# Splitting the query loads from the key loads in layer 1's attention, re-ordering the experts' set-up, and moving a gating product from GpSimd to VectorE

## What is computed

```
h = layernorm(x) * (1 + ca) + sa
x = x + ga * attention(h)
h = layernorm(x) * (1 + cb) + sb
x = x + gb * ffn(h)
```

```
norms = jnp.linalg.norm(out, axis=-1)
denom = jnp.maximum(norms.mean(axis=(0, 2)), 1e-05)
proj = (einsum('bhtk,hkd->bhtd', out / denom, Wo) + bo) * gate_val ; proj.sum(axis=1) / H
...
x_attn = layernorm(x) @ attn_w + attn_b + x
g = x_attn.reshape(2, 8, tpe, D)              # 512 tokens for each of 8 experts
y = gelu(g @ w1 + b1) @ w2 + b2
out = gelu(y @ next_w + next_b)
```

## Time and profile before

| | |
|---|---|
| runs | 2066.65, 2069.05, 2069.82 us; median 2069.05 |
| profiled execution | 2068.8 us, its span 2067.0 us |
| granted TensorE clock, mean | 0.944 |
| busy: TensorE / VectorE / ScalarE / GpSimd | 1851.6 / 1314.4 / 1180.1 / 601.1 us |
| attention of layer 1 | about 1255 to 1729 us |
| experts | 1730 us to the end |

### The profile page before, as it was taken

One profiled execution on the slowest core, in us unless ns is written; L12 is line 12 of the kernel. 1 busy time (PEld: TensorE's weight loads), 2 busy tenths in 40 slices (PEclk: granted clock), 3 DMA queues, 4 the chain that ended last, 5 costly groups with the idle time before them and its releaser, 6 DMA issues. The chain is left out here.

```text
span 2067.0 us, 29571 instructions
## 1 busy us (share of the span) xinstructions
PE 1851.6 (90%) x10317; PEld 752.9 (36%) x10317; DVE 1314.4 (64%) x2607; ACT 1180.1 (57%) x1622; POOL 601.1 (29%) x736
## 2 busy tenths in 40 slices
PE   4789999998879999999999987899999985699998
PEld 3323333322234444444444442233333221354443
DVE  5479888888643553553544524888888771757572
ACT  4268788876742432433323323888888665567663
POOL 5657777662110000000001013111111000354654
PEclk8589999999999999999999996999999996799999
DMA  3344554444260000000000031333433304323310
GB/s 114 62 89 118 133 135 108 121 123 102 95 238 11 11 21 2 21 22 1 22 25 22 21 51 42 52 62 73 72 73 62 62 11 149 113 92 111 124 62 31
DMA packets 119666, 147.92 MB, mean 72 GB/s; under 512 B 19810, under 2 KB 102868, under 8 KB 117460
## 3 DMA queue, kind: packets, MB, share of 16 engines
q1 hardware_dynamic: 119508, 145.79, 27.2%
HBM read 100.34 MB, written 45.14 MB: 70 GB/s over the span
## 5 line engine op out<-in xcount | busy, mean ns | idle before, releaser
L824 DVE TENSOR_REDUCE A_M<-A_SM 128x1 f16<-128x512 f32 x1024 | 657.4, 684 | 154.1 <-PE A_SM L1039 152.0
L590 ACT ACTIVATE A_P<-A_ST 128x1024 f32<-128x1024 f32 x512 | 523.5, 1025 | 146.9 <-PE A_ST L1055 143.8
L1039 PE MATMUL A_SM<-A_KT,A_QS 48*128 48x512 f16 x1024 | 358.7, 405 | 59.6 <-DVE A_M L824 53.4
L1582 PE MATMUL B_PA<-B_Hh,B_wh 128*128 128x512 f16 x1024 | 388.4, 379 | 0.0
L1582 PE MATMUL B_PA<-B_Hl,B_wh 128*128 128x512 f16 x1024 | 388.2, 379 | 0.0
L1501 ACT ACTIVATE B_af<-B_PA,B_sv 128x512 f32<-128x512 f32 x192 | 131.9, 687 | 354.8 <-PE B_PA L1582 354.7
L1055 PE MATMUL A_ST<-A_QS,A_KT 49*128 49x512 f16 x1024 | 304.8, 394 | 7.3 <-DMA A_QS<-A_rows 7.2
L1072 PE MATMUL A_AV<-A_P,A_V 128*32 128x512 f32 x2048 | 283.7, 627 | 4.6 <-ACT A_P L590 4.0
L1039 PEld LDWEIGHTS A_SM<-A_KT,A_QS 48*128 48x128 f16 x1024 | 85.1, 94 | 451.6 <-DVE A_M L824 383.0
L1545 DVE TENSOR_SCALAR B_Hh<-B_af 128x512 f16<-128x512 f32 x128 | 58.4, 456 | 281.4 <-ACT B_af L1501 281.4
L1296 POOL TENSOR_TENSOR B_hl<-B_hf,B_hh 128x512 f16<-128x512 f32 x14 | 16.2, 1156 | 519.2 <-ACT B_hh L1312 519.2
(11 more groups left out here) (346 smaller groups left out, 3191.3 us busy)
## 6 DMA issues: line engine op xcount, KB each, us to landing
D_w_st<-in_we_dram SPq DMA_DIRECT2D x16, 1024.0 KB, 5.0
qk<-A_tr SPq DMA_DIRECT2D x58, 256.0 KB, 2.4
A_KT<-qk SPq DMA_DIRECT2D x96, 128.0 KB, 4.5
A_QS<-qk SPq DMA_DIRECT2D x96, 128.0 KB, 5.0
A_w_st<-in_w_ffn_dram SPq DMA_DIRECT2D x32, 352.0 KB, 3.3
A_QS<-A_rows SPq DMA_DIRECT2D x512, 0.5 KB
w_hi<-A_f_hi SPq DMA_DIRECT2D x32, 176.0 KB, 3.4
w_lo<-A_f_lo SPq DMA_DIRECT2D x32, 176.0 KB, 3.5
```

The lines of the kernel that those rows point to most:

```text
L590: nc.scalar.activation(P[:, st, 2 * pair:2 * pair + 2, :], ST[:, u % 2, :, :], ACT.Exp, scale=1.0 / math.sqrt(HD)).then_inc(exp_s, 1)
L824: nc.vector.tensor_reduce(M[G % 2][:, o:o + 1], SM[:, n % 2, :], AX, ALU.max, negate=True).then_inc(max_s, 1)
L1039: nc.tensor.matmul(SM[:, n % 2, :], QS[b % 2][r, 2 * g + pair, tt * 128:tt * 128 + 128], KT[b % 2][r, 2 * g + pair, :], start=True, stop=T ...
L1582: ins = nc.tensor.matmul(out, a, c, start=start and kt == 0 and n_ == 0, stop=stop and kt == kts[-1] and n_ == len(ops) - 1)
```

## The change

Three things change. In AT1, the six query loads of a batch stand at slots 17, 17, 18, 18 (high halves) and 20, 20 (low halves), the six key loads at 23, 23, 24, 24 and 25, 26; each load waits for its own store, and the semaphores hi_st and lo_st become four. Batches 0 and 1 have places of their own in a table that stays. In the experts, the gate of the head outputs is folded into D_rsc (gsc times rsc) and no longer into the weights; the weights are split in three separate pieces; the row of biases is made on two partitions at once (a matmul with two equal columns, a scale that is 0 on the first partition), so the DMA to the second partition is gone; and SyncE issues the load of y ahead of the weights. In `body`, the product of `finish` is taken by VectorE (`gated`), for both q around D_x, GpSimd keeps the sum, both of them ahead of `add_tokens`; D_y2l is no longer interleaved with `add_tokens`; behind the last expert VectorE takes the sum too.

```diff
@@ -127,7 +127,7 @@
                        H0=39, H1=41, H2=49, H3=51, HIGH=(49, 49, 50, 50, 52, 52, 53, 53), LOWS=(56, 56, 57, 57)))
 AT0 |= OUT | dict(P0=(50,), P1=(52,))
 AT1 = placed(-48, dict(STAT=(-38, -37, -35, -34), AGG=-33, ROOT=-32, XN=(-26, -24, -22, -18), T0=-1, T1=1, HH=(0, 2), HL=(1, 3),
-                       QK0=4, QK1=10, QK2=12, QK3=18, V0=20, V1=26, HIGH=(23, 23, 24, 24, 24, 24, 25, 25), LOWS=(25, 25, 26, 26)))
+                       QK0=4, QK1=10, QK2=12, QK3=18, V0=20, V1=26, HIGH=(23, 17, 23, 17, 24, 18, 24, 18), LOWS=(25, 20, 26, 20)))
 AT1 |= OUT
...
-                             ).then_inc(hi_st if which in (KH, QH) else lo_st, 16)
+                             ).then_inc((kh_st, qh_st, kl_st, ql_st)[which], 16)
...
-                sp.wait_ge(hi_st, 32 * (n + 1))
+                sp.wait_ge((kh_st, qh_st)[i % 2], 16 * (n + 1))
...
+            def load_tokens(e):
+                if e >= 2:
+                    sp.wait_ge(x3_s, 2 * (e - 1))
+                q0, q1, t_ = halves(e)
+                for a, q in enumerate((q0, q1)):
+                    sp.dma_start(x2t[e % 2][:, 2 * a:2 * a + 2, :], d["x2_tok"][q, t_, :].rearrange("(t p) c -> p t c", p=128)
+                                 ).then_inc(x_ld[e % 2], 16)
+
+            def load_x(e, y_only=False):
...
+                if not y_only:
+                    load_tokens(e)
...
+            sp.dma_start(gates[:, :], d["gate"].partition_broadcast(128)).then_inc(c_ld[1], 16)
             sp.dma_start(hsel[:, :, :], d["head_of"]).then_inc(c_ld[0], 16)
-            sp.dma_start(gates[:, :], d["gate"].partition_broadcast(128)).then_inc(c_ld[1], 16)
+            sp.dma_start(gcol[:, :], d["gate"].unsqueeze(1)).then_inc(c_ld[3], 16)
+            load_x(0, True)
+            sp.dma_start(wsm[:, :, :, :], d["w_small"].rearrange("a (k p) n -> p a k n", p=128)).then_inc(c_ld[4], 16)
             sp.dma_start(bo[:, :], d["bo"]).then_inc(c_ld[2], 16)
-            sp.dma_start(gcol[:, :], d["gate"].unsqueeze(1)).then_inc(c_ld[3], 16)
-            sp.dma_start(wsm[:, :, :, :], d["w_small"].rearrange("a (k p) n -> p a k n", p=128)).then_inc(c_ld[4], 16)
+            sp.dma_start(rowf[:, 1, :], d["next_b"].partition_broadcast(2)).then_inc(c_ld[7], 16)
             sp.dma_start(vec[:, :, :], d["vec"].rearrange("a p f -> p a f")).then_inc(c_ld[5], 16)
-            sp.dma_start(rowf[:, 1, :], d["next_b"].unsqueeze(0)).then_inc(c_ld[7], 16)
-            load_x(0)
+            load_tokens(0)
             load_rows(0)
             load_w(0, 0)
             load_w(0, 1)
             sp.dma_start(eb[:, :, :], d["eb"].rearrange("e p f -> p e f")).then_inc(c_ld[6], 16)
-            sp.wait_ge(row_low, 1)
-            sp.dma_start(row2[1:2, :, :], rowl[:, :, :]).then_inc(row_ld, 16)
...
+                    if m == E8 - 1:
+                        sp.wait_ge(x4_last, q_ + 1)
+                    else:
+                        sp.wait_ge(x4_s, 2 * m + q_ + 1)
...
-            def finish(m, qs):
-
-                for q in qs:
+            def finish(m):
+
+                for q in range(2):
                     v = xo[m % 2][:, 2 * q:2 * q + 2, :]
-                    pool.wait_ge(of_s, 2 * m + q + 1)
-                    nc.gpsimd.tensor_tensor(v, v, rows[(m // 2) % 3][:, q, GB, :].unsqueeze(1).to_broadcast([128, 2, C]),
-                                            ALU.mult).then_inc(og_s, 1)
                     pool.wait_ge(og_s, 2 * m + q + 1)
...
-                    finish(m - 1, (0,))
+                    finish(m - 1)
                 if e is not None:
                     add_tokens(e, 0)
                 if m is not None:
                     for f in range(FT):
                         pool.wait_ge(y2_out, FT * m + f + 1)
                         nc.gpsimd.tensor_tensor(y2l[:, f, :], y2f[:, f, :], y2h[:, f, :], ALU.subtract).then_inc(y2_low, 1)
-                        if e is not None and f == 0:
-                            add_tokens(e, 1)
-                elif e is not None:
+                if e is not None:
                     add_tokens(e, 1)
                 if e is not None:
                     root_of(2 * e)
-                if m is not None and m >= 1:
-                    finish(m - 1, (1,))
-                if e is not None:
                     root_of(2 * e + 1)
                 if b + 2 < E8:
                     prepare(b + 2)
-                if m == E8 - 1:
-                    finish(m, (0, 1))
...
-            act.wait_ge(c_ld[7], 16)
-            act.wait_ge(bob_s, 1)
-            nc.scalar.activation(row2[0:1, :, :], rowf[:, :, :], ACT.Copy, scale=WS).then_inc(row_high, 1)
-            act.wait_ge(c_ld[4], 16)
-            act.wait_ge(c_ld[5], 16)
-            act.wait_ge(gsel, 3)
-            act.wait_ge(bT_mm, 1)
-            for f in range(FT):
-                nc.scalar.activation(wsm[:, 0, f, :], wsm[:, 0, f, :], ACT.Copy, scale=gsc[:, f:f + 1]).then_inc(cw_sc, 1)
-                nc.scalar.activation(wsm[:, 1, f, :], wsm[:, 1, f, :], ACT.Copy, scale=vec[:, 0, f:f + 1]).then_inc(cw_sc, 1)
-            act.wait_ge(cw_sc, 2 * FT)
-            nc.scalar.activation(wsh[:, :, :, :], wsm[:, :, :, :], ACT.Copy, scale=WS).then_inc(cw_high, 1)
+            def constants():
+
+                act.wait_ge(ones_s, 5)
+                act.wait_ge(c_ld[7], 16)
+                act.wait_ge(bob_s, 1)
+                nc.scalar.activation(rowh[:, :, :], rowf[:, :, :], ACT.Copy, scale=second_row[:, 0:1]).then_inc(row_high, 1)
+                nc.scalar.activation(wsh[:, 2, :, :], wsm[:, 2, :, :], ACT.Copy, scale=WS).then_inc(cw_high, 1)
+                act.wait_ge(vec_s, 1)
+                for f in range(FT):
+                    nc.scalar.activation(wsh[:, 1, f, :], wsm[:, 1, f, :], ACT.Copy, scale=vec_ws[:, f:f + 1]).then_inc(cw_high, 1)
 
             def prepare(e):
 
                 if e == 0:
-                    act.wait_ge(nsel, 3)
+                    act.wait_ge(nsel, 4)
                 act.wait_ge(y_ld[e % 2], 64 * (e // 2 + 1))
                 for f in range(FT):
                     v = yT[e % 2][:, f, :, :]
                     nc.scalar.activation(v, v, ACT.Copy, scale=rsc[:, f:f + 1]).then_inc(y_sc, 1)
-                if e >= 1:
+                if e == 0:
+                    act.wait_ge(c_ld[4], 16)
+                    nc.scalar.activation(wsh[:, 0, :, :], wsm[:, 0, :, :], ACT.Copy, scale=WS).then_inc(cw_high, 1)
...
+            nc.vector.tensor_tensor(rsc[:, :], rsc[:, :], gsc[:, :], ALU.mult).then_inc(nsel, 1)
+            dve.wait_ge(cw_high, 1)
+            nc.vector.scalar_tensor_tensor(out=wsl[:, 0, :, :], in0=wsm[:, 0, :, :], scalar=WS, in1=wsh[:, 0, :, :],
+                                           op0=ALU.mult, op1=ALU.subtract).then_inc(cw_low, 1)
+            dve.wait_ge(bsum, 1)
+            nc.vector.tensor_copy(rowf[:, 0, :], X[0:2, 1, 0:C]).then_inc(bob_s, 1)
+            dve.wait_ge(row_high, 1)
+            nc.vector.scalar_tensor_tensor(out=row2[:, :, :], in0=rowf[:, :, :], scalar=WS, in1=rowh[:, :, :],
+                                           op0=ALU.mult, op1=ALU.subtract).then_inc(row_low, 1)
...
+            def gated(m, q):
+
+                v = xo[m % 2][:, 2 * q:2 * q + 2, :]
+                dve.wait_ge(of_s, 2 * m + q + 1)
+                nc.vector.tensor_tensor(v, v, rows[(m // 2) % 3][:, q, GB, :].unsqueeze(1).to_broadcast([128, 2, C]),
+                                        ALU.mult).then_inc(og_s, 1)
...
+                        if m is not None and m >= 1:
+                            gated(m - 1, q)
                         dve.wait_ge(z_mm, 2 * e + q + 1)
...
+                if m == E8 - 1:
+                    for q in range(2):
+                        v = xo[m % 2][:, 2 * q:2 * q + 2, :]
+                        gated(m, q)
+                        dve.wait_ge(og_s, 2 * m + q + 1)
+                        nc.vector.tensor_tensor(v, v, x3[m % 4][:, 2 * q:2 * q + 2, :], ALU.add).then_inc(x4_last, 1)
...
+            pe.wait_ge(ones_s, 5)
+            pe.wait_ge(nred, 1)
+            nc.tensor.matmul(X[:, 0, 0:H], ones[:, :], nsum[:, :], start=True, stop=True).then_inc(ntot, 1)
             pe.wait_ge(gcol_s, 1)
             pe.wait_ge(c_ld[2], 16)
-            nc.tensor.matmul(X[0:1, 1, 0:C], gcol[:, :], bo[:, :], start=True, stop=True).then_inc(bsum, 1)
+            nc.tensor.matmul(X[0:2, 1, 0:C], gcol2[:, :], bo[:, :], start=True, stop=True).then_inc(bsum, 1)
...
-            pe.wait_ge(row_ld, 16)
+            pe.wait_ge(row_low, 1)
...
+                if e == 0:
+                    pe.wait_ge(cw_low, 2 + FT)
```

## The result

The changed kernel takes 2042.77 us (median of 5 runs, 2035.09 to 2044.36), the kernel before 2066.69 (5 runs, 2060.17 to 2069.82): ratio 0.989 (0.986 to 0.991), 23.9 us less. Of the 8.2 us between forecast and time, 6.0 are the gain. The rest is my base: I subtracted from the 2069.05 of three runs, 2.4 above the median here. The profiled execution took 2044.36 us, its span 2042.6 against 2067.0.

The account below looks back on a forecast made before the run. TensorE waiting for maxima in layer 1's attention, a DMA of the bias row in the set-up, VectorE and GpSimd in the bodies. 5.2 + 6.5 + 5.0 + 1.2 = 17.9 us off 2068.8: 2050.9, taken as 2051; range 2044 to 2059.

Parts of the forecast that it names:

- part 1: Layer 1's attention: moving query loads out of the burst removes waits for maxima; 5.2 us saved, ends 0 and 5.2.
- part 2: Experts' set-up: first projection at 1742.1 instead of 1749.10, 7.0 us; 6.5 taken, ends 7.5 and 3.
- part 3: Expert bodies e = 3 to 7: products moved to VectorE, 1.0 us each, 5.0; plus 1.2 behind the last gelu.
- They are paid in full: Waits for maxima in layer 1's attention cost full length: 53.92 with 0.48, 55.46 with 2.02, 53.44 without either.
- rival 1: TensorE's clock in layer 1's attention comes back without the wait: up to 3.5 us more saved, 2047.5; chance 0.20.
- the fall may only move: Layer 1's attention, against the clock coming back: it also fell later in that batch with no such wait.
- the 0.5 that I had taken off: Experts' set-up: 6.5 us taken instead of 7.0, since two paths end together with five hand-overs.
- the tail: Behind the last gelu: two GpSimd operations of 1.3 us become two on VectorE of 0.69; 1.2 us saved.
- rival 5: Slower: four query loads delay small DMAs of slot 19 in six batches of layer 1's attention; 2084; chance 0.04.
- 2 to 4: Set-up data late, 2054.5 (0.12); GpSimd's queue eats the bodies' gain, 2056 (0.10); attention's load burst effectively unshrunk, 2056 (0.06).

Follow-up runs that it names:

- e6: Kernel before, with the new query-load slots for the loads of batch 7 alone; 2063.37 us, ratio 0.998.
- e7: Kernel before, with the new query-load slots for the loads of batches 2 to 6 alone; 2060.14 us, ratio 0.998.
- e12: Changed kernel with five waits for the maxima made by hand (SyncE sends small DMAs late in batches 1 to 5); 2063.76 us, ratio to before 0.999.
- e14: Changed kernel with the second add_tokens between the two D_y2l and a shorter, reordered experts' set-up; 2036.15 us, ratio 0.986.
- e9: Changed kernel with the second add_tokens between the two D_y2l again; 2039.44 us, ratio 0.988.
- e11: Changed kernel with the finish sum for q = 1 between the two root_of again; 2038.99 us, one run.
- e0: Changed kernel once more, nothing edited; 2043.83 us, ratio to the kernel before 0.990.
- e13: Changed kernel with the old AT1 and semaphores, so without the moved loads in layer 1's attention; 2052.73 us, ratio 0.994.
- e8: Kernel before, with two more DRAM-to-DRAM transfers of 128 KB in each load burst of batches 2 to 6; 2065.83 us, ratio 1.000.

## Why the forecast was too small

Three stretches, as mean and range over the profiles with the part and without it:

| stretch | without | with | gain | forecast |
|---|---|---|---|---|
| part 1: first to last A_ysb of layer 1 | 419.6 (416.1 to 423.1), 7 | 411.4 (409.4 to 413.4), 8 | 8.2 | 5.2 |
| part 2: first issue to first projection | 19.4 (18.6 to 20.3), 8 | 12.9 (12.5 to 13.7), 9 | 6.5 | 6.5 |
| part 3: second D_x of e = 2 to the end | 249.2 (248.8 to 249.4), 8 | 242.0 (240.4 to 243.2), 6 | 7.2 | 6.2 |

(The last number of a cell is the count of profiles. e6, e7 and e12 change the attention in other ways and stand in the lower rows only; e14, with another set-up, is not in the second, and e9 to e11 and e14, with other bodies, are not in the third.)

**Part 1: the step that failed.** I sized it by the waits alone, "I take 5.2 us", and gave the clock a chance of 0.20. It gave 8.2 +- 1.1. The waits removed were 6.0 us in the mean of seven profiles (7.6 in all, less the 1.64 that stays). I had said "They are paid in full", and they are not: ahead of the 25th A_ysb the two profiles first compared gain 2.0 us (323.6 to 321.6), where five waits of 3.15 us in all went, and without a wait four groups take 53.67 us from A_ysb to A_ysb, not the 53.44 that I had worked out. I put that down to ScalarE, which has to finish its own work ahead of A_ysb, but have not tested it. So 1.1 of the 6.0 do not count, which leaves 4.9. The other 3.3 go to the clock: rival 1, of the size that I had put to it (up to 3.5).

The granted clock agrees: over this stretch its mean is 0.952 to 0.975 in the seven profiles without the part and 0.975 to 0.987 in the eight with it, from which I work out 28 us at the 1.2 GHz level in the mean, against 17. But the size is uncertain: 2.1 +- 1.0 of the 8.2 lie behind the 27th A_ysb, where no wait was removed and only the clock differs, and whether that comes from the part or from chance these profiles can't tell.

e12 shows the mechanism, that the clock falls at such a wait, five times out of five. But the wait is not the only thing that brings it down: from the 25th to the 27th A_ysb, the stretch of the longest wait, all 8 profiles with the wait (e7 too) spend some time at the lower level, and 5 of 10 without it (e6 and e12 too) do so as well (e0: 16.5 us instead of 12.7 from 1634.58). Without the wait it takes 27.6 us in the mean, with it 31.1, a gain of 3.5 for waits of 1.9. So the gain is a mean, and my objection, that the fall may only move, was half right. By the Trainium skill, page "TensorE: Matmul & The Clock Gate", section "What's actually happening", the half clock is the default that activity lifts; e12 agrees, with 0.56 and 0.59 behind the wait where it was 1.00 ahead of it.

A name was wrong too: the six waits stand at the third group of batches 1 to 6, not at the first pair of batches 2 to 7; it is the loads ahead of them that belong to batches 2 to 7.

**Part 2: right in size, in part by luck.** 6.5 us in the mean; the first pair of profiles shows 6.1. But I had the first projection 11.6 us behind the start of the phase, where it comes after 12.9 in the mean, and the start that I compared with was the shortest of its kind, 18.6 where the mean is 19.4; with the 0.5 that I had taken off without a row, these cancel. The row and not y's halves is last, by 0.6 us: D_row took 1.38 us for an operation that I had put at 0.65, and that takes 0.67 in the kernel before, while D_yl ran on GpSimd (1729.12 to 1731.39). The Trainium skill, page "SBUF — State Buffer", section "SBUF: two separate sides", says that of such a pair, which shares a port pair, the one that starts first keeps the other out; the trace agrees: D_row ends 0.6 us behind D_yl, which is about its own length.

**Part 3: right in mechanism, 1.0 too small.** The second tokens are 0.84 us late, not 1.0, D_ht gives back the 2.0, and a body gains 1.25, not 1.0; of this 1.16 is explained (2.0 less 0.84) and 0.09 not traced. Five bodies make 6.2, and the tail 0.9 where I had 1.2 (VectorE's last two operations take the 1.4 us that I gave them). e11 prices the collision by itself, 1.0 us for 1.27 of GpSimd, and e9 the lateness, 0.74.

**The rest.** Of rival 5, a wait at the small DMAs of slot 19, nothing is there. The three stretches give 21.9 us. Over all runs the change measures 23.2 +- 1.3 (17 runs of the changed kernel, mean 2042.6, and 98 of the one before), so 1.3 are left within the error. Whether the parts help one another stays open: alone they give 19.4 +- 3.1 by the means, and e13 can't tell. Of the rivals, 2 to 4 did not come; D_gl does hold the first product up (1.24 us instead of 0.68), in VectorE's idle time.

## What to carry to other kernels

Price a wait of the engine that sets the pace by the clock behind it too: here waits of 2 us cost 4, while waits of 0.4 to 1.1 us cost less than their length. Before an operation goes from GpSimd to VectorE, look at two things: what runs beside it on the other engine, and what its result now makes wait in GpSimd's queue; here they were worth 2.0 and 0.8 us a body with opposite signs, and putting one `add_tokens` back in its place took the second away. Where executions spread by 28 us, a pair of profiles explains its own difference and not the change's; measure the same stretch in many, and take the base of a forecast from many runs: three of them put mine 3 us too high.

## What was not expected of the hardware

- Two more transfers of 128 KB between places in DRAM (e8) left the waits behind the burst as they were (6.5 us in all), and moving six of the twelve loads of 128 KB, which all write to 16 partitions, took them away. So it is not the number of bytes alone that holds the small DMAs up; which limit it is was not tried.
- The granted clock varies from one execution of a kernel to the next (means of 0.939 to 0.956 in the 98 runs of the kernel before), and the time with it, by 28 us. Slow stretches of 14 to 17 us for eight steps come behind waits and without them.
